# The first batch's features in two passes of eight heads, with the second pass and the next batch's projection behind the first chunks of scores

## The reference, cut to what matters

```python
q1 = (bg @ W1_q.T).reshape(B, T, H, 4)      # bg = [x, x shifted by one row]; H = 16
q2 = (bg @ W2_q.T).reshape(B, T, H, 4)
k1 = (x @ W1_k.T).reshape(B, T, H, 4)
k2 = (x @ W2_k.T).reshape(B, T, H, 4)
# plucker_lines: six terms p1[i]*p2[j] - p1[j]*p2[i], divided by their norm
q = _plucker_lines(q1, q2); k = _plucker_lines(k1, k2)
logits = einsum('bhtc,bhsc->bhts', q, k @ _J6.T) * 6.0 ** -0.5
attn = softmax(causal(logits)); o = einsum('bhts,bhsd->bhtd', attn, v)
x = layernorm(x + o @ Wo.T + bo)
```

## Time and profile before

| | |
|---|---|
| median of 3 runs | 990.3 us (988.67 to 993.97) |
| span of the profiled execution | 846.3 us |
| median less span, what lies around the span | 144.0 us |
| attention (span up to about 540 us) | 16 batches |
| PE, DVE, POOL, ACT busy | 84%, 77%, 72%, 69% of the span |

### The profile page before, as it was taken

How to read it: one execution, slowest core, us unless ns; L and a number is a source line. 1 busy time by engine, 2 the same in 40 slices (tenths; PEclk the granted TensorE clock), 3 DMA queues, 4 the chain that set the end, 5 groups by cost and what they waited for, 6 DMA issues and landing times.

```text
span 846.3 us, 23791 instructions
## 1 busy us (share of the span) xinstructions
PE 713.0 (84%) x7568; PEld 455.1 (54%) x7568; DVE 652.2 (77%) x1712; ACT 585.3 (69%) x907; POOL 605.9 (72%) x901
## 2 busy tenths in 40 slices
PE   2689998899998998899999988886899999999700
PEld 2334554454544554445545543475788888887600
DVE  7647798988789889788798794689667666665795
ACT  1478897688786886687887887553466666665456
POOL 4436666689887987698898887653177777777585
PEclk8689999899999999899999998899999999999955
DMA  7000111111111111101201102622663333331496
GB/s 255 14 14 13 38 39 38 52 56 47 51 59 41 50 56 36 58 28 53 68 31 50 45 32 85 210 89 77 170 189 96 100 109 103 102 98 53 121 277 200
DMA packets 88797, 69.89 MB, mean 83 GB/s; under 512 B 8292, under 2 KB 77158, under 8 KB 88720
## 3 DMA queue, kind: packets, MB, share of 16 engines
q1 hardware_dynamic: 69456, 43.43, 17.8%
q0 software_dynamic: 8512, 17.06, 6.1%
q10 hardware_dynamic: 10752, 8.39, 3.3%
HBM read 38.16 MB, written 31.21 MB: 82 GB/s over the span
## 4 chain that ended last, share of the span: by engine, by line
PE 54%; DVE 25%; issue 9%; ACT 6%; POOL 5%; DMA 1%; DVEq 0%; ACTq 0%; POOLq 0%
PE S L905 14%; PE O L727 12%; PE O L927 8%; PE S L712 7%; PE W L686 4%; ACT probs L1071 3%; PE W L752 3%; POOL probs L540 2%; DVE prodA L1276 2%; PE W L662 2%; PE W L943 2%; POOL prodB L528 1%; DVE stats L1686 1%; DVE hid L1634 1%; DVE hid L1613 1%
## 5 line engine op out<-in xcount | busy, mean ns | idle before, releaser
L1071 ACT ACTIVATE probs<-S 128x1024 f32<-128x1024 f32 x320 | 322.7, 1044 | 95.5 <-PE S L712 70.3
L540 POOL TENSOR_SCALAR_AFFINE_SELECT probs<-probs 128x256 f32<-128x256 f32 (+1 forms) x448 | 228.8, 541 | 101.1 <-ACT probs L1071 100.5
L619 POOL DMA_INDIRECT z_scratch<-y,rows x136 | 139.2, 1023 | 63.5 <-issue 36.9
L727 PE MATMUL O<-probs,v_aug 128*32 128x512 f32 (+3 forms) x2048 | 172.9, 458 | 11.9 <-POOL probs L540 11.9
L263 POOL DMA_INDIRECT rows_scratch<-xrow,slot_i x128 | 131.7, 1029 | 44.6 <-issue 27.8
L712 PE MATMUL S<-qkT 32*128 32x512 f16 (+3 forms) x1024 | 137.6, 311 | 17.6 <-ACT probs L1071 9.7
L1634 DVE TENSOR_TENSOR hid<-hid 128x512 f16<-128x512 f32 x100 | 69.3, 693 | 72.4 <-ACT hid L1203 72.4
L1184 ACT ACTIVATE silu<-S 128x512 f32<-128x512 f32 x100 | 59.7, 597 | 91.3 <-PE S L905 90.7
L905 PE MATMUL S<-xT_rt,w_T 128*128 128x256 f16 (+1 forms) x864 | 103.5, 267 | 2.3 <-DVE xT_rt L1595 1.7
L927 PE MATMUL O<-w_T,hid 128*128 (+1 forms) x1200 | 91.5, 221 | 15.1 <-DVE hid L1634 11.7
L712 PEld LDWEIGHTS S<-qkT 32*128 32x128 f16 x1024 | 39.1, 92 | 112.1 <-issue 40.6
(11 more groups left out here) (158 smaller groups left out, 1131.7 us busy)
## 6 DMA issues: line engine op xcount, KB each, us to landing
rows<-rows_scratch SPq DMA_DIRECT2D x64, 130.0 KB
z<-z_scratch SPq DMA_DIRECT2D x32, 256.0 KB, 4.1
xT<-in_x_cols ACTq DMA_DIRECT2D x16, 256.0 KB, 2.8
x_in<-in_L_attn_x ACTq DMA_DIRECT2D x16, 256.0 KB, 3.1
x_scratch<-x SPq DMA_DIRECT2D x16, 256.0 KB, 2.6
x1T_scratch<-x1T SPq DMA_DIRECT2D x16, 256.0 KB, 2.2
xT_sh<-x1T_scratch SPq DMA_DIRECT2D x16, 256.0 KB, 4.4
x_in<-x_scratch SPq DMA_DIRECT2D x16, 256.0 KB, 5.0
```

The costliest lines, as they stand in the source:

```text
L540: pool.affine_select(out=v, in_=v, compare_op=ALU.is_ge, fill=0.0, base=0, pattern=[[0, v.shape[1]], [1, P]], channel_multiplier=-1).then_ ...
L619: pool.indirect_dma_start(out=z_dram, in_=y[:, q, a, :], in_offset=None, out_offset=bass.IndirectOffsetOnAxis(ap=rows[:, q, a, P + 1:P + 2 ...
L727: mm = pe.matmul(O[g % 2][32 * j:32 * j + 32, kb * P:T], v_aug[:, par, kb, 4 * g + j, :], probs[:, g % 2, c, col:col + T - kb * P], start= ...
L1071: act.activation(probs[:, g % 2, c, :], S[(g + c) % 2][:, :], ACT.Exp, scale=-SCALE / SPLIT_UP ** 2).then_inc(s_exp, 1)
```

## The change

The features of batch 0 are computed for heads 0 to 7 and then for heads 8 to 15, on POOL (products) and on DVE (all else), by the same formulas on patterns of half as many elements. One scaling instruction becomes two in each pass, and two copies become three. PE transposes groups 0 and 1 once the first pass is done, and the loop begins. The order on DVE is: first pass, value bias, products of the second pass, copies of groups 0 and 1, the rest of the second pass, `add_bias(0, 0)`, small constants, copies of groups 2 and 3. In `body(0)` PE does the scores (0,0) to (0,3), transposes group 2, scores (0,4), transposes group 3, the first half of the projection of batch 1, scores (1,0), the second half, scores (1,1), the values, then (1,2) and on as before. ACT copies the two halves of the points behind the exponentials of (0,4) and (1,0). POOL's order of masks and products in `body(0)` is unchanged.

```diff
--- before.py
+++ after.py
...
@@ -265,19 +265,26 @@
...
-        def products(dst, many, one):
...
             for i, l0, n in ((0, 0, 3), (1, 3, 2), (2, 5, 1)):
-                yield d[:, 0, :, l0:l0 + n], q_many[:, :, i + 1:4], spread(q_one[:, :, i:i + 1], 2, n)
+                yield d[:, 0, :, :, l0:l0 + n], q_many[:, :, :, i + 1:4], spread(q_one[:, :, :, i:i + 1], 3, n)
             for j, l0, n in ((1, 0, 1), (2, 1, 2), (3, 3, 3)):
-                yield d[:, 1, :, l0:l0 + n], spread(k_many[:, :, j:j + 1], 2, n), k_one[:, :, 0:n]
+                yield d[:, 1, :, :, l0:l0 + n], spread(k_many[:, :, :, j:j + 1], 3, n), k_one[:, :, :, 0:n]
...
@@ -539,7 +546,11 @@
...
-            line_products(0)
+            pool.wait_ge(pts_read, 2)
+            for dst, many, one in products(prodB, 0, 1, FIRST):
+                pool.tensor_tensor(dst, many, one, ALU.mult).then_inc(prodB_first, 1)
+            for dst, many, one in products(prodB, 0, 1, SECOND_HALF):
+                pool.tensor_tensor(dst, many, one, ALU.mult).then_inc(prodB_done, 1)
...
@@ -676,9 +687,11 @@
             def transpose_feat(c, g):
                 w = W[(g + 1) % 2][:, :].bitcast(FP16).rearrange("p (s n) -> p s n", s=2)
-                if g == 0:
+                if isinstance(c, int) and c == 0:
+                    pe.wait_ge(*((feat_first, 1) if g < 2 else (feat_done, 1)))
+                elif g == 0:
                     pe.wait_ge(feat_done, c + 1)
-                elif g >= 2 or isinstance(c, int) and c == 0:
+                if g >= 2 or isinstance(c, int) and c == 0 and g == 1:
                     pe.wait_ge(featT_read, HP * c + g - 1)
...
@@ -822,15 +835,10 @@
                     scores(b, par, g, (c,))
                 logits(0, 0)
-                if first:
-                    transpose_feat(0, 2)
                 if not last and not first:
                     project_points(b + 1, 1 - par, 0)
                 logits(0, 1)
-                if first:
-                    transpose_feat(0, 3)
-                    project_points(1, 1, 0)
-                if not last:
+                if not last and not first:
                     project_points(b + 1, 1 - par, 1)
                 logits(0, 2)
                 if not first:
@@ -838,16 +846,26 @@
                 logits(0, 3)
                 if not first:
                     weigh(b - 1, 1 - par, 3, (1, 2, 3))
+                if first:
+                    transpose_feat(0, 2)
                 logits(0, 4)
                 if sends(b):
                     ranks(b - 3)
-                if not last:
+                if first:
+                    transpose_feat(0, 3)
+                    project_points(1, 1, 0)
+                elif not last:
                     project_values(b + 1, 1 - par)
                 logits(1, 0)
+                if first:
+                    project_points(1, 1, 1)
+                    logits(1, 1)
+                    project_values(1, 1)
                 if not first:
                     transpose_out(b - 1, 0, not last)
                     transpose_out(b - 1, 1, not last)
-                logits(1, 1)
+                if not first:
+                    logits(1, 1)
                 if not first:
                     transpose_out(b - 1, 2, not last)
                     transpose_out(b - 1, 3, not last)
@@ -1130,18 +1148,26 @@
                     load_columns(b + 2, par)
                     load_x(b + 2, par)
                 exps(b, 0, (0,))
-                if not last:
+                if not last and not first:
                     copy_points(b + 1, 0)
                 exps(b, 0, (1,))
-                if not last:
+                if not last and not first:
                     copy_points(b + 1, 1)
                 exps(b, 0, (2, 3))
                 if not first:
                     copy_out(b - 1, 3)
                 exps(b, 0, (4,))
-                if not last:
-                    copy_values(b + 1, 1 - par)
-                exps(b, 1, (0, 1, 2, 3))
+                if first:
+                    copy_points(1, 0)
+                    exps(0, 1, (0,))
+                    copy_points(1, 1)
+                    exps(0, 1, (1,))
+                    copy_values(1, 1)
+                    exps(0, 1, (2, 3))
+                else:
+                    if not last:
+                        copy_values(b + 1, 1 - par)
+                    exps(b, 1, (0, 1, 2, 3))
                 copy_out(b, 0)
                 exps(b, 1, (4,))
                 if not first:
@@ -1269,48 +1295,68 @@
                 dve.scalar_tensor_tensor(out=wr_T[:, 1, :], in0=wr_cols, scalar=UP, in1=wr_T[:, 0, :], op0=ALU.mult,
                                          op1=ALU.subtract)
-            def line_terms(c):
+            def line_terms(c, heads=slice(0, H)):
                 dve.wait_ge(pts_read, 2 * (c + 1))
-                for dst, many, one in products(prodA, 1, 0):
+                for dst, many, one in products(prodA, 1, 0, heads):
                     ins = dve.tensor_tensor(dst, many, one, ALU.mult)
                 chain(ins)
...
+            def subtract_terms(c, heads=None):
+                if heads is FIRST:
+                    dve.wait_ge(prodB_first, NPROD)
+                else:
+                    dve.wait_ge(prodB_done, NPROD * (c + 1))
+                a, b = lines_of(prodA, heads), lines_of(prodB, heads)
+                chain(dve.tensor_tensor(a, a, b, ALU.subtract))
+            def lines_of(ap, heads):
+                return ap[:, :, :] if heads is None else by_head(ap[:, :, :], heads)
+            def scalars_of(ap, heads):
+                v = ap[:, :].rearrange("p (n o) -> p n o", o=1)
+                return v if heads is None else by_head(v, heads)
...
+            def scale_lines(heads=None):
+                rs = scalars_of(rs_a, heads)
+                if heads is not None:
+                    chain(dve.tensor_scalar(rs, rs, SPLIT_UP * ROOT_SCALE, None, ALU.mult))
+                    chain(dve.tensor_tensor(lines_of(prodB, heads), lines_of(prodA, heads), spread(rs, 3, LINE), ALU.mult))
+                    return
+                rs = spread(rs, 2, LINE)
+                chain(dve.scalar_tensor_tensor(out=lines_of(prodB, heads), in0=lines_of(prodA, heads),
+                                               scalar=SPLIT_UP * ROOT_SCALE, in1=rs, op0=ALU.mult, op1=ALU.mult))
             def write_features(c):
-                rs = spread(rs_a[:, :].rearrange("p (h o) -> p h o", o=1), 2, LINE)
-                chain(dve.scalar_tensor_tensor(out=prodB[:, :, :], in0=prodA[:, :, :], scalar=SPLIT_UP * ROOT_SCALE, in1=rs,
-                                               op0=ALU.mult, op1=ALU.mult))
+                scale_lines()
                 dve.wait_ge(featT_full, HP * c)
-                if isinstance(c, int) and c == 0:
-                    dve.wait_ge(feat_clear, 1)
                 chain(dve.tensor_copy(feat[:, :, 0:LINE], prodB[:, :, :]))
                 dve.tensor_tensor(feat[:, :, LINE:2 * LINE], prodB[:, :, :], feat[:, :, 0:LINE], ALU.subtract)\
                     .then_inc(prodB_read, 1)
@@ -1319,6 +1365,23 @@
...
+            def write_first_features(heads):
+                scale_lines(heads)
+                dve.wait_ge(feat_clear, 1)
+                f = by_head(feat[:, :, :], heads)
+                hi, lo = f[:, :, :, 0:LINE], f[:, :, :, LINE:2 * LINE]
+                chain(dve.tensor_copy(hi, lines_of(prodB, heads)))
+                ins = dve.tensor_tensor(lo, lines_of(prodB, heads), hi, ALU.subtract)
+                if heads is not FIRST:
+                    ins.then_inc(prodB_read, 1)
+                    dve.wait_ge(prodB_read, 1)
+                else:
+                    chain(ins)
+                dve.tensor_copy(f[:, 0:NT, :, 2 * LINE:4 * LINE], f[:, 0:NT, :, 0:2 * LINE])
+                dve.tensor_copy(f[:, NT:, :, 3 * LINE:4 * LINE], hi[:, NT:])
+                dve.tensor_copy(f[:, NT:, :, 2 * LINE:3 * LINE], lo[:, NT:]).then_inc(feat_first if heads is FIRST else feat_done, 1)
...
@@ -1433,18 +1496,26 @@
                     .then_inc(xres_done, 1)
             spread_bias()
-            line_terms(0)
+            line_terms(0, FIRST)
+            subtract_terms(0, FIRST)
+            square_lines(FIRST)
+            sum_squares(FIRST)
+            inverse_norms(FIRST)
+            write_first_features(FIRST)
             add_value_bias()
-            subtract_terms(0)
-            square_lines()
-            sum_squares()
-            inverse_norms()
-            write_features(0)
-            for g in range(HP):
-                copy_feat(0, 0, g)
+            line_terms(0, SECOND_HALF)
+            copy_feat(0, 0, 0)
+            copy_feat(0, 0, 1)
+            subtract_terms(0, SECOND_HALF)
+            square_lines(SECOND_HALF)
+            sum_squares(SECOND_HALF)
+            inverse_norms(SECOND_HALF)
+            write_first_features(SECOND_HALF)
             dve.wait_ge(bo_read, 1)
```

(2 more changed lines are left out.)

49 lines of the change are left out of this document (26 added, 23 removed).

## The result

The changed kernel took 1007.5 us (median of six runs, 995.8 to 1010.5); the kernel before, timed beside it, 994.6 us (six runs, 988.7 to 1001.1). The ratio is **1.0141, 95% interval 1.0102 to 1.0181**: slower by 1.4%. Forecast were 998.0 on 990.3, a ratio of 1.0078, and a range of 992.5 to 1003.5. The sign was right, the time lies above the range. Of the 9.5 us between 998.0 and 1007.5, some 4.3 are the kernel before itself, whose median is 994.6 over six runs and was 990.3 over the first three.

A forecast was written before the change was run, and what follows sets the result against it. It took the path from batch 1's points through POOL's products and masks to first weighing as setting the start: 8.8 us delay less 1.0 for the clock, +7.8 on 990.3, gives 998 us, range 992.5 to 1003.5.

The forecast's parts named there:

- The three times named as signs of being right: Start of the kernel: first exponential at 31 to 33, features of heads 0 to 7 at 20.5 to 22, points at 41 to 44.
- the one in which the clock pays back: Rival at start: points at 39.2, delay 6.0, up to 2.4 us back in weighing; +3.6 us, 994; chance 0.19.
- The one of 1002 us: Rival: low clock throughout and full DVE/POOL exclusion, points at 43.8 + 1.0, no payback; +11.6 us; chance 0.15.
- The faster one: Rival: early chunks work as meant and low-clock stretches of the later loop vanish; 985 us; chance 0.04.
- First pass done: DVE's features of heads 0 to 7: products to 13.1, plus 6.5 and 1.5 us, done at 21.1 us.
- the exclusion beside POOL's second half: DVE's first pass, slowed by POOL's second-half products running beside it: 1.5 us, between 0 and 3.2.
- The full 2.5 us: DVE's first pass under the whole-instruction rule: POOL's entire product time added, ending the pass 1 us later.
- Between the passes: DVE from 21.1 to 24.4 us: value bias 0.3, second-half products 1.0, then copies of PE's transposes of groups 0 and 1.
- Points: ACT's second copy of batch 1's points, behind the late projection: complete at 42.0 us, bounds 40.7 to 43.8 by clock.
- Delay: Batch 1's points: 42.0 instead of 33.2 us, so 8.8 us later, passed on to weighing.
- What may come back: First weighing of the loop: PE's clock may rise sooner with another phase; 1.0 us taken off.
- the 144 us put down as lying around the span: Outside the profiled span: 144.0 us assumed as surroundings, so that the 846.3 us profile stands on the 990.3 us median.

The follow-up runs named there:

- set 4: Idle DVE memsets added on one chip: 8 and 26 to the changed kernel, 35 and 53 to the kernel before; ratios 1.0451, 1.0103, 1.0341, 1.0045.
- f2_after: The changed kernel, unchanged, timed again on another chip against the kernel before: 871.3 us beside 862.3, ratio 1.0110.
- e2_bias_early: Changed kernel with batch 0's bias addition moved up behind the value bias, ahead of the second pass: 978.1 us, ratio 1.0087 to the kernel before.
- e3_proj_early: Changed kernel with two passes kept, batch 1's projection and copies put back among the first two chunks: 967.4 us, ratio 0.9985 to the kernel before.
- f1_pad_before: Kernel before with 27 one-column DVE memsets added in batch 0, where DVE was idle: 861.3 us, ratio 1.0036 to the kernel before.
- g4_pad_ahead: Kernel before with 27 DVE memsets added ahead of batch 0, behind the small constants: 996.2 us, ratio 1.0066 to the kernel before.
- f3_pad_after: Changed kernel with 20 DVE memsets added in batch 0's idle stretch: 864.3 us, ratio 1.0043 to the kernel before.
- e1_before: The kernel before, unchanged, as control on another chip: 969.0 us beside 969.4, ratio 0.9975.
- g3_pad_behind: Kernel before with 27 DVE memsets added behind the whole loop over batches: 995.2 us, ratio 1.0021 to the kernel before.
- h4_before_53: Kernel before with 53 DVE memsets added, nothing moved: ratio 1.0045 to the kernel before.

## Why the prediction was right, and where it failed

**Right, and shown by runs: the structure of the start.** The load behind `xres_done` keeps holding ACT, so the early features serve nothing; weighing follows the points by POOL's products and masks, 6.98 to 7.02 us in every kernel with POOL's order unchanged, but for the 6.26 us of two passes with the early projection; the late projection is what delays the points. The three times named as signs of being right (first exponential at 31 to 33, first features at 20.5 to 22, points at 41 to 44) all came 0.15 to 0.72 us ahead of their windows. Of the rivals, the one in which the clock pays back needed points at 39.2 and an end within 5 us; neither came. The one of 1002 us was nearest in time, yet by a mechanism that did not happen: its points were to come at 44.8 at the lower clock. The faster one is out, and by the early bias it would have been out even with ACT set free.

**The terms, forecast and measured.** First pass done 21.1, measured 20.35: the exclusion beside POOL's second half was put at 1.5 us and is 7.38 - 6.35 = 1.0. The full 2.5 us, the other weighing that I gave, did not appear. (That one was by the Trainium skill, SBUF — State Buffer, on the shared port pair, which has the two exclude each other for a whole instruction; the trace bears out an exclusion, but not one for all of POOL's time.) Second pass 6.5, measured 6.35. Between the passes 3.3, measured 2.8. Bias addition done 31.6, measured 30.07, the sum of these. First exponential 32.0, measured 30.51, just inside the lower bound of 30.3. Points 42.0, measured 40.28, of which 1.5 us is inherited from ACT's start; from there to the points I had 10.0 us and it took 9.8, the clock rising within the first half of the projection as assumed. Delay 8.8, measured 7.1. Weighing 49, measured 47.27.

**The step that failed** is the sum's last, "What may come back": -1.0 us and no other term for the loop, with the sentence that every later batch follows the one before. The start gave +7.1 and the kernel +12.9 between the medians (+14.0 by the ratio), so what follows the start added some 6 to 7 us where I took 1 off. This and the size of the start are 5.1 of the 9.5 us by which the time was off; the other 4.3 us are before's own median, which moved from 990.3 to 994.6. On a median of 990.3 the same +12.9 would have ended at 1003.2, just inside the range, so that the time lies outside it is in part luck. The single size errors at the start ran the other way and hid part of it: with the right delay my own scheme would have said +6.1.

A term that I put at nothing is that of 27 more DVE instructions ahead of a loop. I priced them by their durations alone; set 4 shows that instructions which cost nothing in themselves can cost 0.4% or 3.4%, by how many they are, through the loading of the loop's program. But after has no such stall (31 packets on that queue, as before), so this is not what the change itself paid. **What the 6 to 7 us are stays open.** The kernels with the small gap in batch 4 (after, its repeat `f2_after`, `e2_bias_early`, `e3_proj_early`, `f1_pad_before`, `g4_pad_ahead`) ended on average 3.8 us later than their start shift accounts for (-0.5 to 6.9), the nine others without a stall 0.1 us earlier (-4.0 to 4.1), by the ratios and the weighing of the earlier trace rows. Three kernels stand above their start shift beyond their interval, all with the gap: after, `e2_bias_early` and `g4_pad_ahead`; `f3_pad_after`, without it, stands below. But the groups overlap, and the repeat of after at 1.0110 is within its interval of the start alone, so the gap is a hint and no proof, and part of the excess may be scatter.

**A second misreading** was the 144 us put down as lying around the span. A gap of that size between a profiled execution and the timed runs should have been a question: most likely the two came from different chips, and the stretches behind the start in the earlier trace rows were not those of the chip to be timed. It moved no term of the sum. The granted clock over the loop differs little, 0.95 in the earlier trace rows and 0.95, 0.93 and 0.93 in the same stretch of `e1_before`, `g3_pad_behind` and `h4_before_53`. Most of what differs lies behind the loop: from the last exponential to the end it is 306.8 us in the profile of before and 417.6 in `e1_before`.

**A sign unread** was in the earlier trace rows: the 2427 ns maximum of an instruction whose median is 360. It was the collision with POOL (last section) by which a batch can get several microseconds longer, and it speaks against "later batches follow": a shift of DVE against POOL by a microsecond or two brings it on or ends it.

## What to carry to other kernels

When early results are to start work sooner, follow the queue of the engine that would use them: here a load that waited for the bias addition stood ahead, and what the change moved out of the way (a projection that had run for free in the same idle time) was on the path of the next batch. Instructions added ahead of a large generated loop are not priced by their duration alone; look at the instruction queues in the DMA list of the profile, and time the kernel with a few idle instructions more, before a difference of 1% is put down to an idea. And compare the profiled execution's own time with the timed runs first: if they are far apart, as here by 144 us, their rows come from different conditions.

## What the runs showed of the hardware

- **Position of code on DVE.** One-column memsets that cost nothing where they stand brought after to 1.0451 (8 of them) or 1.0103 (26), and before to 1.0341 (35) or 1.0045 (53). In the two slow ones DVE stood twice for 1.9 to 2.6 us in every second batch, at fixed operations, and in each of the sixteen stalls a packet of 8192 bytes ran on DMA queue 14, which the profile labels "instruction" (51 packets on that queue in the slow ones, 31 or 32 in all others). The places where the small gap fell in batch 4, the 3rd and the 4th operation, came out as the rule of one operation per two instructions had said; what causes that gap was not found.
- **DVE beside POOL.** How long the six products of DVE in the loop take depends on when POOL's own six begin. Over 18 profiles they took 1.4 us in all 124 batches in which POOL's began 1.6 us behind DVE's or later, 3.0 in nearly all in which both began together (batches 1 to 3), and 3.8 to 7.1 in 49 of the 50 in which POOL's began 0.6 to 1.5 us behind, in the middle of DVE's. Two batches of after, in DVE's timeline and then in POOL's:

```profile
415.64 6.91 DVE L1302 TENSOR_TENSOR prodA<-p 128x192 f32<-128x192 f32 x6
...
452.38 1.40 DVE L1302 TENSOR_TENSOR prodA<-p 128x192 f32<-128x192 f32 x6
```

```profile
416.38 0.78 POOL L547 TENSOR_SCALAR_AFFINE_SELECT probs<-probs 128x256 f32<-128x256 f32 x2
417.12 3.14 POOL L535 TENSOR_TENSOR prodB<-p 128x192 f32<-128x192 f32 x6
...
452.02 1.03 POOL L263 DMA_INDIRECT rows_scratch<-xrow,slot_i  x1 [0.30 <-issue]
453.06 1.34 POOL L547 TENSOR_SCALAR_AFFINE_SELECT probs<-probs 128x256 f32<-128x256 f32 x2
454.37 2.94 POOL L535 TENSOR_TENSOR prodB<-p 128x192 f32<-128x192 f32 x6
```

  In the profile of after this happened in batches 6, 8, 10 and 12, in the control `e1_before` in none, in the profile of before in 8 and 10. Which batches are hit varies between the profiles of even near kernels, and blurs any shift of the start by some microseconds. The indirect DMAs are not what holds DVE: the second batch above has one beside DVE's products and takes 1.40 us, and over all profiles a product of the loop beside nothing but an indirect DMA took at most 0.38 us, one beside POOL's products alone up to 2.48.
- **Chips differ.** The same kernel took 862 us on one chip and 969 to 996 us on three others. Ten units in the middle of the expert phase take about 24 us on the first and in the profile of before, and 34 to 42 us on the others. No experiment looked for the cause.
